# A layer with three recurrences: beta times state made by VectorE instead of GpSimd, and the projections' pieces behind the cell's sum

## What is computed

```python
# 1: LSTM over 256 steps, 8 rows of 128
z = xz_t + prev_h @ Wh
i, f, o, g = sigmoid(ai), sigmoid(af), sigmoid(ao), tanh(ag)
next_c = f * prev_c + i * g
next_h = o * tanh(next_c)
# 2: delta rule with a state S of (b=8, h=8, 32, 32); xp = silu(h @ W_in.T); k, v, q, beta from xp
kn = k / (norm(k) + 1e-6)
retrieved = einsum('bhij,bhj->bhi', S, kn)
delta = v - retrieved
S = tanh(beta[..., None] * S + delta[..., None] * kn[..., None, :])
Sq = einsum('bhij,bhj->bhi', S, q)
out = Sq * silu(Sq)                      # then x = x + out @ W_out.T
# 3: a plain recurrence
next_h = tanh(prev_h @ Wh + xW_t)
```

## Time and profile before

| | |
|---|---|
| median of 3 runs | 3503.22 us |
| profiled execution | 3513.58 us |
| its span | 3511.8 us |
| mean granted TensorE clock | 0.640 |
| PE busy | 2892.3 us (82%) |
| DVE busy | 1998.0 us (57%) |
| ACT busy | 1084.7 us (31%) |
| POOL busy | 761.1 us (22%) |
| DMA, mean | 29 GB/s |

### The profile page before, as it was taken

The page is one execution under the profiler, slowest core; times in us unless marked ns, Lnnn a source line. Parts: engine busy times, 40 slices in busy tenths (PEclk is TensorE's granted clock), DMA queues, the critical chain, the costliest instruction groups (busy, mean ns, idle before and its releaser), DMA issues. The chain is left out here.

```text
span 3511.8 us, 94099 instructions
## 1 busy us (share of the span) xinstructions
PE 2892.3 (82%) x35913; PEld 2166.8 (62%) x35915; DVE 1998.0 (57%) x6665; ACT 1084.7 (31%) x4414; POOL 761.1 (22%) x1477
## 2 busy tenths in 40 slices
PE   6889999937888884788888888888546889999998
PEld 3558888834546663555666666565414568888755
DVE  3544444463535443677777777774375854444577
ACT  1233222211222332333334333333223432222222
POOL 1110111102100001444444444445101211111000
PEclk9995555557986895555555555555557965555699
DMA  1000000000000002433433333344000000000000
GB/s 74 2 2 0 0 0 0 0 32 1 2 1 0 1 17 66 90 61 70 90 71 62 78 81 70 64 84 84 37 0 1 2 0 0 0 0 0 0 0 12
DMA packets 106854, 101.32 MB, mean 29 GB/s; under 512 B 95616, under 2 KB 95616, under 8 KB 97536
## 3 DMA queue, kind: packets, MB, share of 16 engines
q1 hardware_dynamic: 106624, 98.13, 12.7%
HBM read 89.68 MB, written 8.39 MB: 28 GB/s over the span
## 5 line engine op out<-in xcount | busy, mean ns | idle before, releaser
L580 POOL TENSOR_TENSOR l2r_beta_s<-l2r_state,l2r_beta_f 128x256 f32<-128x256 f32 x512 | 360.9, 725 | 601.3 <-ACT l2r_state L485 582.8
L375 PE MATMUL l2r_o_ps<-l2r_rows,l2r_outer 32*128 32x128 f32 x2048 | 207.6, 493 | 167.1 <-DVE l2r_rows L687 164.6
L695 DVE TENSOR_TENSOR l2r_pre<-l2r_o_ps,l2r_beta_s 128x256 f32<-128x256 f32 x512 | 193.2, 419 | 151.9 <-PE l2r_o_ps L375 151.1
L375 PEld LDWEIGHTS l2r_o_ps<-l2r_rows,l2r_outer 32*128 32x128 f32 x2048 | 139.2, 306 | 196.0 <-issue 196.0
L475 ACT ACTIVATE l2r_gates<-l2r_lstm_ps 128x24 f32<-128x24 f32 x256 | 48.6, 190 | 643.6 <-PE l2r_lstm_ps L327 643.4
L363 PE MATMUL l2r_d_ps<-l2r_state,l2r_kq 128*32 128x128 f32 x2056 | 199.1, 421 | 11.5 <-ACT l2r_state L485 10.6
L485 ACT ACTIVATE l2r_state<-l2r_pre 128x256 f32<-128x256 f32 x512 | 186.3, 418 | 68.2 <-DVE l2r_pre L695 68.2
L327 PEld LDWEIGHTS l2r_lstm_ps<-l2r_h_ring,l2r_w_part 128*128 128x128 bf16 x3072 | 103.5, 105 | 121.1 <-DVE l2r_h_ring L680 82.7
L665 DVE TENSOR_TENSOR l2r_h_rest<-l2r_h_ring 128x8 f32<-128x8 f32 x256 | 151.6, 592 | 8.7
L133 PE MATMUL l3r_acc<-l3r_xw,main_base 128*128 x512 | 154.7, 389 | 1.6 <-issue 1.6
L133 PE MATMUL l0r_acc<-l0r_xw,main_base 128*128 x512 | 154.4, 388 | 1.6 <-issue 1.6
(11 more groups left out here) (529 smaller groups left out, 7661.5 us busy)
## 6 DMA issues: line engine op xcount, KB each, us to landing
l2r_beta_f<-l2r_beta_store SPq DMA_DIRECT2D x256, 256.0 KB, 5.2
main_odd_layers<-in_l SPq DMA_DIRECT2D x1, 4826.5 KB, 14.0
l2r_beta_store<-l2r_beta_tok SPq DMA_DIRECT2D x256, 8.0 KB, 1.5
main_odd_layers<-in_l SPq DMA_DIRECT2D x1, 3672.0 KB, 15.9
l2r_v_store<-l2r_v_part SPq DMA_DIRECT2D x128, 24.0 KB, 2.0
l2r_v_rows<-l2r_v_store SPq DMA_DIRECT2D x16, 192.0 KB, 6.7
main_decay<-in_decay SPq DMA_DIRECT2D x1, 3072.0 KB, 10.3
main_even_layers<-in_l SPq DMA_DIRECT2D x1, 2762.5 KB, 9.9
```

Of the source, the lines that this page charges most:

```text
L375: last = nc.tensor.matmul(o_ps[:, c, 0:P], outer[chunk_rows(c), n // TC % 2, n % TC, :, :].rearrange("p a b -> p (a b)"), rows[chunk_rows( ...
L580: nc.gpsimd.tensor_tensor(beta_s[:, half], state[:, half], beta_f[:, q % BETA_SLOTS, n % QUARTER, half], ALU.mult).then_inc(s["bs_ready"], 1)
L695: nc.vector.tensor_tensor(pre[:, half].rearrange("p (c n) -> p c n", c=2), o_ps[:, 2 * h:2 * h + 2, 0:P], beta_s[:, half].rearrange("p (c ...
```

## The change

The function `kept` moves from GpSimd to VectorE, in the step behind `masked` (and `add_out`) and ahead of `summed`. `project` and `output` on VectorE move from before `summed` to behind `lstm_cell`, ahead of `lstm_h`. On GpSimd the other work stays in its order. TensorE's queue is the same as before; so are ScalarE's and SyncE's.

```diff
--- before.py
+++ after.py
@@ -570,16 +570,6 @@
 
             @block.gpsimd
             def _(pool):
-                def kept(n):
-                    q = n // QUARTER
-                    if n % QUARTER == 0:
-                        pool.wait_ge(beta_loaded[q % BETA_SLOTS], 16 * 4 * (q // BETA_SLOTS + 1))
-                    for h in range(2):
-                        half = slice(h * 2 * P, (h + 1) * 2 * P)
-                        pool.wait_ge(state_ready[h], n + 1)
-                        nc.gpsimd.tensor_tensor(beta_s[:, half], state[:, half], beta_f[:, q % BETA_SLOTS, n % QUARTER, half],
-                                                ALU.mult).then_inc(s["bs_ready"], 1)
-
                 def spread(src, mask, slots, which, g, h, t0, count):
                     here = src.rearrange("p (b t) -> p t b", t=TC)[:, t0:t0 + count, h * BH:(h + 1) * BH]
                     return nc.gpsimd.tensor_tensor(kq[:, slots:slots + count, 2 * h + g, which, :, :],
@@ -643,8 +633,6 @@
                 for k in range(BODIES + 1):
                     lstm, proj, delta, out, rnn = waves(k)
                     for step in range(TC):
-                        if delta is not None:
-                            kept(delta * TC + step)
                         if proj is not None:
                             project(proj, step)
                         if out is not None:
@@ -679,6 +667,16 @@
                         dve.wait_ge(s["xin_psum"], n // TC - 1)
                     nc.vector.tensor_tensor(h_ring[:, n % SLOTS, :], gates[:, 2 * B:3 * B], tanh_c[:, :],
                                             ALU.mult).then_inc(s["h_ready"], 1)
+
+                def kept(n):
+                    q = n // QUARTER
+                    if n % QUARTER == 0:
+                        dve.wait_ge(beta_loaded[q % BETA_SLOTS], 16 * 4 * (q // BETA_SLOTS + 1))
+                    for h in range(2):
+                        half = slice(h * 2 * P, (h + 1) * 2 * P)
+                        dve.wait_ge(state_ready[h], n + 1)
+                        nc.vector.tensor_tensor(beta_s[:, half], state[:, half], beta_f[:, q % BETA_SLOTS, n % QUARTER, half],
+                                                ALU.mult).then_inc(s["bs_ready"], 1)
 
                 def masked(n):
                     dve.wait_ge(s["d_psum"], n + 1)
@@ -782,15 +780,17 @@
                             masked(n)
                         if rnn is not None and step == 0:
                             add_out(rnn)
+                        if delta is not None:
+                            kept(n)
+                            summed(n)
+                        if lstm is not None:
+                            lstm_both(lstm * TC + step)
+                            lstm_cell(lstm * TC + step)
                         if proj is not None:
                             project(proj, step)
                         if out is not None:
                             output(out, step)
-                        if delta is not None:
-                            summed(n)
                         if lstm is not None:
-                            lstm_both(lstm * TC + step)
-                            lstm_cell(lstm * TC + step)
                             lstm_h(lstm * TC + step)
                         if lstm is not None and lstm * TC + step + 1 < T:
                             part_rest(lstm * TC + step + 1)
```

## The result

The change makes the kernel faster: 3459.97 us, the median of 4 runs (3458.44 to 3469.72), against 3503.71 for the kernel before (4 runs, 3497.37 to 3512.38). The ratio is 0.9875 (95% interval 0.9857 to 0.9894). The profiled execution took 3469.72 us (span 3467.9), 43.9 less than that of before. The prediction was 3457 us, range 3420 to 3490.

The account below looks back on a forecast made before the run. A chain of waits, stretched by GpSimd's products, was taken to bound the steps. 45 us less over 13 bodies, 6 less in the first with a state and 5 more elsewhere gave 46; scaled, 3457 us, range 3420 to 3490.

Parts of the forecast that it names:

- What bounds the step: Each step: a chain of waits; GpSimd's products stretch h_ring and h_rest by 0.23 + 0.48 us, 0.55 reaching the mask.
- Products at no cost: VectorE behind the mask (start M): a pair occupies some 0.70 us, additions stay at M+1.30, cover 0.35, path cost nothing.
- Pieces behind the cell's sum: VectorE, before h_ring: pieces fill the wait for tanh_c; up to 0.55 us fits before the next mask is later.
- The two waits of TensorE: TensorE waits for xp in step 2 (0.72 us later) and for the output's transpose in step 12 (1.15 later).
- Rival B: Steps with pieces: starting 0.3 us later loses 2.7 of the 3.45 us a body; 3492 us, no change; 10%.
- Steps 5 to 8: 17.24 becomes 16.0 us: 7.5 for steps 5 and 6, 4.05 for 7, 4.4 for 8 with GpSimd's square.
- Steps 9 to 11: 13.10 becomes 11.65 us (4.05, 3.35, 4.25); GpSimd's spreads charged 0.7 in step 9 and 0.85 in step 11.
- Rival C: Stalls charged to GpSimd don't fall on the chain: 2.7 us more gained a body, 3422 us; 12%.
- Rival A: GpSimd's remaining work falls on the chain in full: 9.1 us more a body, 3576 us, slower; 5%.
- Rival D: Nothing changes, because the next mask waits for TensorE anyway; 3%.
- Body 2: First body with a state (67.70 us), without reductions or output: some 6 us less.
- Bodies 16 and 17 and the start: Bodies without a cell recurrence and the one before the state starts pay for TensorE's waits: 5 us more.

## Why the prediction was right, and where its terms were off

- **What bounds the step.** Right. Step 1 was predicted from the rows of before to 0.04 us; the groups above and the tanh in PSUM, which takes away only the contention at h_ring, show the stretching to be the cause.
- **Products at no cost.** Right where GpSimd rests: 0.75 for a pair, additions at M+1.30. The cover of 0.35 us was tested by doubling them (0.2 us a step then). The group's mean is 469 ns and not 424, because pairs beside GpSimd's spreads took 1.32 and 1.52 us, as shown below for steps 9 and 11.
- **Pieces behind the cell's sum.** The two waits of TensorE were predicted at +0.72 and +1.15 over the TensorE-bound period; steps 2 and 12 came out within 0.04. The idle time shown is 0.53 and 0.95, less than the 0.7 and 1.1 named as signs. Rival B (3492), that pieces delay every step, did not come: one reduction fits in the wait for tanh_c. Its price counted nine steps with pieces, but there are ten (1 to 8, 11 and 12), which makes 3.0 us a body and not 2.7.
- **Steps 5 to 8, 16.0 predicted and 16.71 measured: the term that was mis-sized most.** It has two parts. I had VectorE's two reductions end step 5 (and 7.5 for steps 5 and 6); TensorE did. The timeline after:

```profile
1887.33 1.20 PE L397 MATMUL l2r_m_ps<-main_even_layers,l2r_xp 128*128 128x256 f32 x2
...
1888.54 0.64 PE L363 MATMUL l2r_d_ps<-l2r_state,l2r_kq 128*32 128x128 f32 x8
...
1889.26 0.29 DVE L685 TENSOR_TENSOR l2r_rows<-l2r_d_ps,main_even_layers 128x128 f32<-128x128 f32 x1 [0.22 <-PE l2r_d_ps L363]
```

  The projection of step 5 stands in TensorE's queue as that of step 2 does, so the period is 3.87 (steps 5 and 6: +0.25). In step 8 (+0.53) the square holds h_rest, as charged, but the spreading of q stands right behind it in GpSimd's queue and holds the next instruction too:

```profile
1900.45 1.04 POOL L616 TENSOR_TENSOR l2r_sq_sq<-l2r_sq 128x512 f32<-128x512 f32 x1 [14.31 <-PE l2r_d_ps L363]
1901.45 3.75 POOL L575 TENSOR_TENSOR l2r_kq<-l2r_q_f,main_even_layers 128x240 f32<-128x240 f32 x8
```

```profile
1900.48 1.03 DVE L653 TENSOR_TENSOR l2r_h_rest<-l2r_h_ring 128x8 f32<-128x8 f32 x1
1901.55 0.62 DVE L648 TENSOR_TENSOR l2r_h_low<-l2r_h_rest 128x8 bf16<-128x8 f32 x1
...
1902.30 1.32 DVE L678 TENSOR_TENSOR l2r_beta_s<-l2r_state,l2r_beta_f 128x256 f32<-128x256 f32 x2
```

  h_rest takes 1.03, then h_low 0.62; the experiment with the square on ScalarE takes 0.89 us off this step.
- **Steps 9 to 11, 11.65 predicted and 11.33 measured.** The 0.7 charged for the spreads of q in step 9 fell in part into step 8 (h_low's 0.45), the rest on the products (1.32 in place of 0.75), which put the additions 0.15 later, the cover taking the remainder, and on the cell's sum behind them, which took 0.62. Steps 8 and 9 together were 8.64, against 8.45. Step 11 (4.28, against 4.25) shows the keys' spreads on the products, 1.52 for the pair:

```profile
1909.36 1.52 DVE L678 TENSOR_TENSOR l2r_beta_s<-l2r_state,l2r_beta_f 128x256 f32<-128x256 f32 x2
1910.80 0.74 DVE L693 TENSOR_TENSOR l2r_pre<-l2r_o_ps,l2r_beta_s 128x256 f32<-128x256 f32 x2
```

- **Rival C** (the charges don't fall on the chain, 3422) did not come: the spreads and the square cost what was charged, and a little more. **Rival A** (3576) acts in steps 4, 8, 9 and 11 alone, as charged. **Rival D** can't hold with step 1 at 3.31.
- **Body 2.** 6 us less predicted, 5.0 measured. The miss is the wait for v of 3.6 us, where I had looked at the loads of beta only; the body's other steps gained more than I had counted (its step 0 fell from 5.41 to 4.84). TensorE's far longer wait for the first v, 10.64 us before and 9.24 after, stands in both traces, so it is hardly part of the difference, but the prediction did not look at it either.
- **Bodies 16 and 17 and the start.** 5 more predicted; 2.1, 1.1 and 1.1 measured. The last figure, the later start of the delta rule, doesn't belong to the change: the stage's first h_ring came 1.05 us later too (1314.16 against 1313.11), and from there to the first mask it is 92.3 us in both. Over all profiled executions that first h_ring lies anywhere from 1302.4 to 1314.2 us, so work ahead of the stage varies by up to 12 us; why is open.

The errors are +0.7, -0.3 and otherwise 0.1 or less in a body: the sum was right partly because they cancel, which is luck, and the direction because each step was bounded by a row. The step table also adds up to 3.49 us less in a body, where the prediction writes 3.45; over 13 bodies that is half a microsecond.

## What to carry to other kernels

When GpSimd and VectorE work at the same time, compare the duration of VectorE's small two-operand instructions with those where GpSimd rests; where they are stretched, first move one of the operands to PSUM, which took a few lines here and gained twice what the change did (92 against 44 us). Pieces of other work that are to fill gaps need a place for each step: ahead of the chain's instruction where another engine's queue waits for them, behind it otherwise. A loop made shorter makes transfers late that were hidden, so look at what its loads had to spare.

## What the runs showed of the hardware

- A short VectorE instruction with two SBUF inputs that starts during a GpSimd instruction ends when that one ends: in the trace before, the 225 h_ring that start well inside one all end 0.02 to 0.03 us after it. The next is held by the next one even where GpSimd's instructions stand back to back: h_rest 1.03 and h_low 0.62 beside the square (1.04) and the spreads that follow, 0.17 each without. The Trainium skill, "SBUF — State Buffer", section "Who interferes with whom", tells of the contention, and the trace agrees.
- With longer instructions the two engines take turns: beside the spreads, products of 0.42 us take 0.95 and end 0.28 after the spread they started beside, and a spread of 0.74 takes 0.92 and ends 0.60 after the product before it.
- With one operand in PSUM the same operation is free of it: h_ring 163 ns in the mean, against 406, with as many GpSimd products beside it.
